# A two-layer recurrence: two of four k tiles of the recurrent product in bf16 parts, x Wx + b added behind the transpose

## The chip, the core and the metric

The kernel runs on one core of a Trainium2 chip. The metric is the device time of one execution in microseconds (us).

## The reference

Input x is (8, 1024, 512) in f32: 8 sequences (B) of 1,024 steps (T) and width 512 (D). Two layers, each with its own Wx and Wh (512 x 512) and b, start from the same state cond (8 x 512):

```
def step(h_prev, xw_t):
    h_next = jnp.tanh(h_prev @ Wh + xw_t)      # xw_t = x_t @ Wx + b
    return (h_next, h_next)
x = x + layer0(x, cond, Wx0, Wh0, b0)
x = x + layer1(x, cond, Wx1, Wh1, b1)
return x
```

So 2 x 1,024 steps depend on one another within each layer; layer 1's input at step n needs layer 0's output at step n.

## The kernel before

Everything is f32 but the bias. The width of 512 is held as 128 partitions times 4 k tiles (KC = 4). Layer 1 runs 8 steps (LAG) behind layer 0, so in a "slot" s the kernel does step s of layer 0 and step s - 8 of layer 1; 1,016 of the 1,032 slots hold both layers, 8 at each end hold one.

**TensorE.** The small operand, h or x of four steps (32 columns: 4 steps x 8 sequences), is loaded into a 32-column group of the array; the 128 columns of a piece of W stream past it. The four column groups g take the four quarters of the output width and write PSUM partitions 32g to 32g + 31, so four matmuls, one for each g, run side by side. `project` (L184) computes x Wx of four steps at once, one k tile in each call (L192), and for k = 0 first adds the bias with one bf16 matmul for each g (L188); it starts the accumulation in a PSUM bank `ps`, of which each layer has two. `recur` (L199) waits for the last h (L203) and adds h Wh into the same bank, with 16 matmuls (4 k tiles x 4 groups, L206); h of step n - 1 stands in a window of 32 columns of which 24 are zeros, placed so that it lands in the rows of step n. `slot` (L211) writes the order out: recur of layer 0, a projection step, one or more projection steps of layer 1 by a table (L30), recur of layer 1.

**VectorE** waits for the recurrence (`turn`, L275) and transposes the whole bank in 32 x 32 blocks into `zt` (L277). Every four slots it also does two sums of four steps each: `sum_mid`, x + h of layer 0, which is layer 1's input (L282), and `sum_out`, x_mid + h of layer 1, the output (L287). **ScalarE** waits for the transpose and applies tanh to the 32 columns of its step, which gives h (`tanh`, L244, L257). **GpSimd** only clears h at the start (L271). **SP** (SyncE) moves 64 KB pieces of four steps: x for TensorE, x for VectorE, and the output (L165 to L175). The programs of TensorE, ScalarE and VectorE are loops over eight slots (`stretches`, L54) with the first and last slots written out; the class `Edge` keeps their semaphore counts. At the start VectorE splits the bias in three bf16 parts (L305 to L315).

## Time and profile before

| | |
|---|---|
| median of 3 runs | 2303.1 us (2302.53 to 2303.13) |
| profiled execution, its own time | 2300.86 us |
| its span in the trace | 2299.1 us |
| TensorE busy / its weight loads | 99% / 99% |
| VectorE / ScalarE / GpSimd busy | 33% / 21% / 0% |
| granted TensorE clock | 1.0 of full speed |
| HBM traffic | 24 GB/s over the span |

PE is TensorE's matmul, PEld its weight load, DVE is VectorE, ACT ScalarE, POOL GpSimd, SP SyncE. Matmuls are pipelined and their ends are modelled, so that TensorE is "busy" does not say that it works at its peak. A line of a kernel is written L206.

### The profile page before, as it was taken

The numbers are of one execution on the slowest core, as the hardware profiler recorded it, in microseconds if no ns is written. First come the engines' busy times: TensorE is split into PE (matmuls) and PEld (weight loads), VectorE is DVE, ScalarE is ACT, GpSimd is POOL, SyncE is SP. The second block draws the span as 40 slices with busy tenths as digits, with TensorE's granted clock in tenths as the row PEclk, the third lists the DMA queues.
The fourth block names the chain that finished last, engine by engine and source line by source line (L and its number), as shares of the span: only waits on it lengthen the run. The fifth ranks groups of instructions, "written<-read, shape, count | busy, mean of one in ns | idle before, by whom it ended". The sixth has DMA issues, their size and how long they took to land.

```text
span 2299.1 us, 176381 instructions
## 1 busy us (share of the span) xinstructions
PE 2272.2 (99%) x83968; PEld 2264.9 (99%) x83968; DVE 759.5 (33%) x2573; ACT 471.4 (21%) x2049; POOL 2.2 (0%) x6
## 2 busy tenths in 40 slices
PE   6999999999999999999999999999999999999998
PEld 6999999999999999999999999999999999999998
DVE  2333333333333333333333333333333333333332
ACT  1222222222222222222222222222222222222221
POOL 0000000000000000000000000000000000000000
PEclk9999999999999999999999999999999999999999
DMA  2000000000000000000000000000000000000000
GB/s 100 26 22 23 22 23 22 23 22 23 22 23 22 23 22 23 22 23 22 23 22 23 22 23 22 23 22 23 22 23 22 23 22 23 22 23 22 23 22 18
DMA packets 112545, 55.61 MB, mean 24 GB/s; under 512 B 13440, under 2 KB 111744, under 8 KB 112000
## 3 DMA queue, kind: packets, MB, share of 16 engines
q1 hardware_dynamic: 112368, 54.08, 7.9%
q10 hardware_dynamic: 144, 1.05, 0.1%
q8 instruction: 25, 0.41, 0.1%
q14 instruction: 8, 0.07, 0.0%
HBM read 38.31 MB, written 16.78 MB: 24 GB/s over the span
## 4 chain that ended last, share of the span: by engine, by line
PE 99%; DVE 0%; DMA 0%; ACT 0%; issue 0%; SPq 0%; ACTq 0%; DVEq 0%
PE ps L206 78%; PE ps L192 20%; PE ps L188 1%; DMA bias<-b_in 0%; DVE zt L277 0%; ACT h L257 0%; DVE bias_rest L307 0%; DVE bias_last L311 0%; DVE bias_part L315 0%; DVE bias_part L313 0%; DVE bias_part L309 0%; SPq L156 0%; SPq L155 0%; SPq L154 0%; DVE x_out L287 0%
## 5 line engine op out<-in xcount | busy, mean ns | idle before, releaser
L206 PE MATMUL ps<-wh,h 128*32 128x128 f32 x65536 | 2103.9, 273 | 7.8 <-ACT h L257 7.4
L206 PEld LDWEIGHTS ps<-wh,h 128*32 128x32 f32 x65536 | 1956.7, 110 | 14.5 <-ACT h L257 11.9
L277 DVE STREAM_TRANSPOSE zt<-ps 128x128 f32<-128x128 f32 x2048 | 649.0, 317 | 1489.3 <-PE ps L206 1489.3
L257 ACT ACTIVATE h<-zt 128x32 f32<-128x32 f32 x2048 | 470.1, 230 | 1824.1 <-DVE zt L277 1824.1
L192 PE MATMUL ps<-wx,x_pe 128*32 128x128 f32 x8192 | 563.2, 273 | 0.0
L192 PE MATMUL ps<-wx,x_mid 128*32 128x128 f32 x8192 | 478.1, 273 | 0.0
L192 PEld LDWEIGHTS ps<-wx,x_pe 128*32 128x32 f32 x8192 | 383.0, 110 | 0.2
L192 PEld LDWEIGHTS ps<-wx,x_mid 128*32 128x32 f32 x8192 | 339.5, 110 | 0.0
L188 PE MATMUL ps<-bias_part,ones 128*32 128x128 bf16 x2048 | 198.2, 219 | 16.1 <-DVE bias_part L315 16.1
L188 PEld LDWEIGHTS ps<-bias_part,ones 128*32 128x32 bf16 x2048 | 114.0, 97 | 16.1 <-DVE bias_part L315 16.1
L282 DVE TENSOR_TENSOR x_mid<-x_dve,h 128x128 f32<-128x128 f32 x256 | 74.8, 292 | 37.4 <-DVE x_out L287 0.2
L287 DVE TENSOR_TENSOR x_out<-x_mid,h 128x128 f32<-128x128 f32 x256 | 63.9, 250 | 0.3 <-ACT h L257 0.3
L307 DVE TENSOR_TENSOR bias_rest<-bias 128x512 f32<-128x512 f32 x2 | 1.4, 694 | 9.6 <-DMA bias<-b_in 9.5
L271 POOL MEMSET h<- 128x1096 f32 x2 | 2.0, 1011 | 0.3 <-POOLq L344 0.3
L257 ACT ACT_TABLE_LOAD x1 | 1.3, 1283 | 1.2 <-PEq L344 1.2
L311 DVE TENSOR_TENSOR bias_last<-bias_rest 128x512 f32<-128x512 f32 x2 | 1.3, 673 | 0.0
L313 DVE COPY bias_part<-bias_rest 1x512 bf16<-1x512 bf16 x2 | 0.8, 418 | 0.1
L315 DVE CAST bias_part<-bias_last 1x512 bf16<-1x512 f32 x2 | 0.8, 418 | 0.0
L309 DVE COPY bias_part<-bias 1x512 bf16<-1x512 bf16 x2 | 0.8, 407 | 0.0
L317 DVE MEMSET ones<- 128x32 bf16 x1 | 0.1, 85 | 0.8 <-PEq L344 0.8
L318 DVE MEMSET bias_part<- 128x256 uint32 x1 | 0.3, 272 | 0.0
L319 DVE MEMSET bias_part<- 128x256 uint32 x1 | 0.3, 272 | 0.0
(4 smaller groups left out, 0.4 us busy)
## 6 DMA issues: line engine op xcount, KB each, us to landing
x_pe<-x_t SPq DMA_DIRECT2D x256, 64.0 KB, 1.8
x_dve<-x_t SPq DMA_DIRECT2D x256, 64.0 KB, 1.9
out_t<-x_out SPq DMA_DIRECT2D x256, 64.0 KB, 1.7
wx<-wx_in SPq DMA_DIRECT2D x2, 1024.0 KB, 7.6
wh<-wh_in ACTq DMA_DIRECT2D x1, 1024.0 KB, 5.7
wh<-wh_in SPq DMA_DIRECT2D x1, 1024.0 KB, 9.3
bias<-b_in SPq DMA_DIRECT2D x2, 256.0 KB, 8.2
h<-cond_t SPq DMA_DIRECT2D x2, 16.0 KB, 8.1
```

The lines of the kernel that those rows point to most:

```text
L188: pe.matmul(bank(l, c, g), ones[:, :], bias_part[l][:, g * P:(g + 1) * P], start=True, stop=False, skip_group_check=True, tile_position=(0 ...
L192: mm = pe.matmul(bank(l, c, g), src, wx[l][:, k, g * P:(g + 1) * P], start=False, stop=False, skip_group_check=True, tile_position=(0, 32 ...
L206: mm = pe.matmul(bank(l, n // S4, g), h[l][:, at + k * ROWS:at + (k + 1) * ROWS], wh[l][:, k, g * P:(g + 1) * P], start=False, stop=k == K ...
L257: act.activation(h_of(l, n), src[:, :, off:off + B], ACT.Tanh).then_inc(done, 1)
L271: pool.memset(h[l][:, :], 0.0).then_inc(s_clear, 1)
L277: dve.transpose(zt[l][n % 2][:, :], ps[l][n // S4 % 2][:, 0:P]).then_inc(zt_done[l].sem, 1)
L282: dve.tensor_tensor(x_group(x_mid, c), x_group(x_dve, c), h_group(0, c), ALU.add).then_inc(mid_last if c == NG - 1 else mid_done.sem, 1)
L287: dve.tensor_tensor(x_group(x_out, c), x_group(x_mid, c), h_group(1, c), ALU.add).then_inc(out_own.sem, 1)
L307: dve.tensor_tensor(bias_rest[l][:, :], bias[l][:, :], upper(bias[l][:, :]), ALU.subtract).then_inc(s_bown, 1)
L309: dve.tensor_copy(bias_part[l][0:1, :], upper(bias[l][0:1, :]))
L311: dve.tensor_tensor(bias_last[l][:, :], bias_rest[l][:, :], upper(bias_rest[l][:, :]), ALU.subtract).then_inc(s_bown, 1)
L313: dve.tensor_copy(bias_part[l][32:33, :], upper(bias_rest[l][32:33, :]))
```

## The change

- **Two k tiles in bf16 parts.** For k = 0 and 1, Wh is split before the loop into three bf16 parts (`wh_part`: upper half of the number, upper half of the rest, last rest), and h of each step into three parts too. The parts of h stand beside each other in 24 columns (3 parts x 8 sequences) and are loaded together, as the upper halves of f32 words; the three parts of Wh stream past them in turn, which gives all nine products, in 24 rows of each group. k = 2 and 3 stay in f32 and run first, as soon as h is there; k = 2 with 32 columns (the columns behind the first 8 hold zeros there), which also starts all 32 rows, k = 3 with 8. TensorE waits a second time, for the parts (`split_done`), before the bf16 matmuls: 6 for each column group, 24 in a step, in the place of 8 f32 ones.
- **Own banks.** The recurrence accumulates in `ps_rec`, one bank for each layer, the projections in `ps_xw`, two for each layer.
- **Behind the transpose.** VectorE transposes the recurrence's bank into columns 8 to 39 of a slot of `zt`, and once per layer and four steps the projections' bank into columns 0 to 7 of four slots (`place`). A `tensor_reduce` (`total`) adds up four pieces of 8 columns: x Wx + b and the three rows of parts. ScalarE's tanh reads the sum `z`.
- **Splitting h** on VectorE: `rest` (h less its upper half) after tanh, `last` (rest less its upper half), for two k tiles of 8 columns: 16 elements each. VectorE's order of these operations is written out in `slot`.
- **The two sums** go from VectorE to GpSimd. GpSimd also makes the parts of layer 1's Wh at the start; VectorE and ScalarE make those of layer 0.
- **Projections** are spread two k tiles a slot, one behind each layer's recurrence. **SP** has the store ahead of the x_dve load, and loads layer 1's Wh earlier. VectorE's and ScalarE's loops are written out; only TensorE keeps one.

The core of the diff:

```diff
+KB = 2
+PARTS = 3
...
+LAYERS = (0, 1)
...
-        wh = [sb(f"wh{l}", [P, KC, D]) for l in LAYERS]
+        wh = [sb(f"wh{l}", [P, KC * D]) for l in LAYERS]
+        wh_rest = [sb(f"wh_rest{l}", [P, KB * D]) for l in LAYERS]
+        wh_part = [sb(f"wh_part{l}", [P, PARTS, KB * D], BF16) for l in LAYERS]
...
-        h = [sb(f"h{l}", [P, 2 * HALF + B]) for l in LAYERS]
-        zt = [[sb(f"zt{l}_{i}", [P, P]) for i in range(2)] for l in LAYERS]
...
+        h = [sb(f"h{l}", [P, RING * P]) for l in LAYERS]
+        zt = [sb(f"zt{l}", [P, RING * KC * SLOT]) for l in LAYERS]
+        z = [[sb(f"z{l}_{i}", [P, COLS]) for i in range(2)] for l in LAYERS]
...
-        ps = [[ctx.enter_context(nc.psum_tensor(f"ps{l}_{i}", [P, 512], F32)) for i in range(2)] for l in LAYERS]
+        ps_rec = [psum(f"ps_rec{l}") for l in LAYERS]
+        ps_xw = [[psum(f"ps_xw{l}_{i}") for i in range(2)] for l in LAYERS]
...
+        h_done = [sem(f"h_done{j}") for j in range(2)]
+
+        def h_count(l, n):
+
+            s = n + LAG * l
+            steps = [(m, t) for t in range(s - s % S4, s + 1) for m in LAYERS if number(m, t) is not None]
+            return h_done[s // S4 % 2], steps.index((l, s)) + 1
...
-        def window(n):
-
-            w = n % RING
-            return w // 4 * HALF + w % 4 * P + (32 if w % 4 == 3 else 0), B * ((n + 1) % 4)
+        def h_step(l, n):
+            return h[l][:, n % RING * P:(n % RING + 1) * P].rearrange("p (k c) -> p k c", k=KC)
 
         def h_of(l, n):
-            at, off = window(n)
-            return h[l][:, at:at + P].rearrange("p (k r) -> p k r", r=ROWS)[:, :, off:off + B]
+            return h_step(l, n)[:, :, 0:B]
+
+        def h_bits(l, n):
+
+            return h[l][:, n % RING * P:(n % RING + 1) * P].bitcast(BF16).rearrange(
+                "p (k c two) -> p k c two", k=KC, two=2)[:, :, :, 1]
 
...
+            sp.dma_start(wh[1][:, :], weights[1][1].rearrange("p k d -> p (k d)")).then_inc(s_wh[1], DMA)
...
-            sp.dma_start(wh[1][:, :, :], weights[1][1]).then_inc(s_wh[1], DMA)
             for c in range(1, NG + 4):
-                if c + 1 in range(2, NG):
-                    sp.wait_ge(s_x_pe_used, c)
+                if 2 <= c + 1 < NG:
+                    sp.wait_ge(proj_done[0], c)
                     load(x_pe, x_pe_loaded, c + 1)
-                if c in range(2, NG):
-                    sp.wait_ge(s_x_mid_seen, c - 1)
+                if c >= 4:
+                    sp.wait_ge(out_done, c - 3)
+                    sp.dma_start(out[:, c - 4, :], x_out[c % 2][:, :]).then_inc(out_free[c % 2], DMA)
+                if 2 <= c < NG:
+                    sp.wait_ge(mid_done, c - 1)
                     load(x_dve, x_dve_loaded, c)
-                if c >= 4:
-                    sp.wait_ge(s_out_done, c - 3)
-                    sp.dma_start(out[:, c - 4, :], x_out[c % 2][:, :]).then_inc(out_free[c % 2].sem, DMA)
...
+                bank = ps_xw[l][c % 2]
                 if k == 0:
...
                 for g in range(QG):
-                    mm = pe.matmul(bank(l, c, g), src, wx[l][:, k, g * P:(g + 1) * P], start=False, stop=False,
-                                   skip_group_check=True, tile_position=(0, 32 * g))
...
+                    mm = pe.matmul(rows(bank, g, ROWS), src, wx[l][:, k, g * P:(g + 1) * P], start=False,
+                                   stop=k == KC - 1, skip_group_check=True, tile_position=(0, 32 * g))
+                if k == KC - 1:
+                    mm.then_inc(proj_done[l], 1)
 
             def recur(l, n):
 
-                at, _ = window(n - 1)
-                if n:
-                    h_done.wait(pe, h_at[l, n - 1])
-                for k in range(KC):
+
+                if n == 0:
+                    pe.wait_ge(s_hinit, 2 * DMA)
+                else:
+                    pe.wait_ge(*h_count(l, n - 1))
+                for k in range(KB, KC):
+                    m = ROWS if k == KB else B
                     for g in range(QG):
-                        mm = pe.matmul(bank(l, n // S4, g), h[l][:, at + k * ROWS:at + (k + 1) * ROWS],
-                                       wh[l][:, k, g * P:(g + 1) * P], start=False, stop=k == KC - 1,
-                                       skip_group_check=True, tile_position=(0, 32 * g))
-                mm.then_inc(rec_done.sem, 1)
-
-            def slot(r):
-
+                        at = k * D + g * P
+                        pe.matmul(rows(ps_rec[l], g, m), h_step(l, n - 1)[:, k, 0:m], wh[l][:, at:at + P],
+                                  start=k == KB, stop=False, skip_group_check=True, tile_position=(0, 32 * g))
+                if n == 0:
+                    pe.wait_ge(s_hsplit, 2)
+                    pe.wait_ge(s_wpart[l], PARTS)
+                else:
+                    pe.wait_ge(split_done, SPLIT_AT[l, n - 1] - base)
+                for k in range(KB):
+                    for i in range(PARTS):
+                        for g in range(QG):
+                            at = k * D + g * P
+                            mm = pe.matmul(rows(ps_rec[l], g, PARTS * B), h_bits(l, n - 1)[:, k, 0:PARTS * B],
+                                           wh_part[l][:, i, at:at + P], start=False,
+                                           stop=k == KB - 1 and i == PARTS - 1, skip_group_check=True,
+                                           tile_position=(0, 32 * g))
+                mm.then_inc(rec_done, 1)
...
+            def projections(s, half):
+
+                l, k = s % S4 // 2, s % 2 * 2 + half
+                c = (s - 6) // S4 if l else s // S4 + 1
+                if 0 <= c < NG:
...
+                    project(l, c, k)
+
+            def slot(s):
+
+                if (n := number(0, s)) is not None:
+                    recur(0, n)
+                projections(s, 0)
+                if (n := number(1, s)) is not None:
+                    recur(1, n)
+                projections(s, 1)
...
-                        mid_done.wait(act, c + 1)
-                zt_done[l].wait(act, n + 1)
-                src = zt[l][n % 2][:, :].rearrange("p (k r) -> p k r", r=ROWS)
-                off = B * (n % S4)
-                done = h_last[l] if n == T - 1 else h_done.sem
-                act.activation(h_of(l, n), src[:, :, off:off + B], ACT.Tanh).then_inc(done, 1)
...
+                        act.wait_ge(mid_done, c + 1)
+                elif n % S4 == 0 and n >= RING:
+                    act.wait_ge(out_done, n // S4 - 1)
+                act.wait_ge(z_done, STEP_AT[l, n])
+                act.activation(h_of(l, n), z[l][n % 2][:, :].rearrange("p (k b) -> p k b", k=KC), ACT.Tanh).then_inc(
+                    h_count(l, n)[0], 1)
...
+                if s % S4 == 0 and s:
+                    done, count = h_count(*last)
+                    act.sem_inc(done, -count)
...
+            act.activation(wh_part[0][:, 0, :], upper(wh[0][:, 0:KB * D]), ACT.Copy).then_inc(s_wpart[0], 1)
+            act.wait_ge(s_wrest[0], 1)
+            act.activation(wh_part[0][:, 1, :], upper(wh_rest[0][:, :]), ACT.Copy).then_inc(s_wpart[0], 1)
...
+            def sum_mid(c):
+
+                pool.wait_ge(x_dve_loaded[c % 2], DMA * (c // 2 + 1))
+                if c >= 2:
+                    pool.wait_ge(out_done, c - 1)
+                pool.wait_ge(rest_done, STEP_AT[0, S4 * c + 3])
+                pool.tensor_tensor(x_group(x_mid, c), x_group(x_dve, c), h_group(0, c), ALU.add).then_inc(mid_done, 1)
...
+            def sum_out(c):
...
+                pool.wait_ge(mid_done, c + 1)
+                pool.wait_ge(rest_done, STEP_AT[1, S4 * c + 3])
+                pool.tensor_tensor(x_group(x_out, c), x_group(x_mid, c), h_group(1, c), ALU.add).then_inc(out_done, 1)
...
+            pool.wait_ge(s_wh[1], DMA)
+            full, rest = wh[1][:, 0:KB * D], wh_rest[1][:, :]
+            pool.tensor_tensor(rest, full, upper(full), ALU.subtract).then_inc(s_wrest[1], 1)
+            pool.tensor_copy(wh_part[1][:, 0, :], upper(full)).then_inc(s_wpart[1], 1)
+            pool.wait_ge(s_wrest[1], 1)
+            pool.tensor_copy(wh_part[1][:, 1, :], upper(rest)).then_inc(s_wpart[1], 1)
+            pool.tensor_tensor(wh_part[1][:, 2, :], rest, upper(rest), ALU.subtract).then_inc(s_wpart[1], 1)
...
+            def place(l, c):
...
+                dve.wait_ge(proj_done[l], c + 1)
+                dve.transpose(zt_group(l, c), ps_xw[l][c % 2][:, 0:P]).then_inc(xw_done[l], 1)
...
             def turn(l, n):
-                rec_done.wait(dve, rec_at[l, n])
-                dve.transpose(zt[l][n % 2][:, :], ps[l][n // S4 % 2][:, 0:P]).then_inc(zt_done[l].sem, 1)
-
...
+                dve.wait_ge(rec_done, STEP_AT[l, n])
+                dve.transpose(zt_of(l, n)[:, :, B:SLOT], ps_rec[l][:, 0:P]).then_inc(zt_done, 1)
+
+            def total(l, n):
+                if n % S4 == 0:
+                    dve.wait_ge(xw_done[l], n // S4 + 1)
+                dve.wait_ge(zt_done, STEP_AT[l, n])
+                dve.tensor_reduce(z[l][n % 2][:, :].rearrange("p (k b) -> p k b", k=KC),
+                                  zt_of(l, n)[:, :, 0:4 * B].rearrange("p k (i b) -> p k b i", b=B),
+                                  AX.X, ALU.add).then_inc(z_done, 1)
...
+            def rest(l, n):
+                step = h_step(l, n)
+                return dve.tensor_tensor(step[:, 0:KB, B:2 * B], step[:, 0:KB, 0:B], h_bits(l, n)[:, 0:KB, 0:B],
+                                         ALU.subtract)
...
+            def last(l, n):
+                step = h_step(l, n)
+                return dve.tensor_tensor(step[:, 0:KB, 2 * B:3 * B], step[:, 0:KB, B:2 * B],
+                                         h_bits(l, n)[:, 0:KB, B:2 * B], ALU.subtract)
+
+            def split_rest(l, n):
+                dve.wait_ge(*h_count(l, n))
+                rest(l, n).then_inc(rest_done, 1)
...
+            def split_last(l, n):
+                if n < T - 1:
+                    dve.wait_ge(rest_done, STEP_AT[l, n])
+                    last(l, n).then_inc(split_done, 1)
+
+            def slot(s):
+                a, b, b_before = number(0, s), number(1, s), number(1, s - 1)
+                if a is not None:
+                    turn(0, a)
+                if b_before is not None:
+                    split_last(1, b_before)
+                if a is not None:
+                    total(0, a)
+                    if s % S4 == 2 and s // S4 + 1 < NG:
+                        place(0, s // S4 + 1)
+                if s % S4 == 0 and s >= LAG and b is not None:
+                    place(1, b // S4)
+                if a is not None:
+                    split_rest(0, a)
+                if b is not None:
+                    turn(1, b)
+                if a is not None:
+                    split_last(0, a)
+                if b is not None:
+                    total(1, b)
+                    split_rest(1, b)
...
+            dve.wait_ge(s_wh[0], DMA)
+            w_full, w_rest = wh[0][:, 0:KB * D], wh_rest[0][:, :]
+            dve.tensor_tensor(w_rest, w_full, upper(w_full), ALU.subtract).then_inc(s_wrest[0], 1)
+            dve.wait_ge(s_hinit, 2 * DMA)
+            rest(0, -1)
+            rest(1, -1).then_inc(s_hsplit, 1)
+            dve.wait_ge(s_wrest[0], 1)
+            dve.tensor_tensor(wh_part[0][:, 2, :], w_rest, upper(w_rest), ALU.subtract).then_inc(s_wpart[0], 1)
+            dve.wait_ge(s_hsplit, 1)
```

## Rows read from the trace of the kernel before

**Rows 1.** The page, busy time of each engine: us, share of the span, instructions.

```profile
PE 2272.2 (99%) x83968; PEld 2264.9 (99%) x83968; DVE 759.5 (33%) x2573; ACT 471.4 (21%) x2049; POOL 2.2 (0%) x6
```

**Rows 2.** The page, chain that ended last: by engine, then by line.

```profile
PE 99%; DVE 0%; DMA 0%; ACT 0%; issue 0%; SPq 0%; ACTq 0%; DVEq 0%
PE ps L206 78%; PE ps L192 20%; PE ps L188 1%; DMA bias<-b_in 0%; DVE zt L277 0%; ACT h L257 0%; DVE bias_rest L307 0%; DVE bias_last L311 0%; DVE bias_part L315 0%; DVE bias_part L313 0%; DVE bias_part L309 0%; SPq L156 0%; SPq L155 0%; SPq L154 0%; DVE x_out L287 0%
```

**Rows 3.** Busy time of each engine in a stretch of two-layer slots (x: instructions).

```profile
core 0: us, PE busy (x) PEld busy (x) DVE busy (x) ACT busy (x) POOL busy (x), PEclk, DMA share, GB/s
1000.00:1100.00 100.00, 100.00 (x3719) 100.00 (x3714) 33.33 (x114) 20.66 (x90) 0.00 (x0) 1.00 0.08 22
```

**Rows 4.** The page, groups: xcount | busy, mean ns | idle before, releaser.

```profile
L206 PE MATMUL ps<-wh,h 128*32 128x128 f32 x65536 | 2103.9, 273 | 7.8 <-ACT h L257 7.4
...
L277 DVE STREAM_TRANSPOSE zt<-ps 128x128 f32<-128x128 f32 x2048 | 649.0, 317 | 1489.3 <-PE ps L206 1489.3
L257 ACT ACTIVATE h<-zt 128x32 f32<-128x32 f32 x2048 | 470.1, 230 | 1824.1 <-DVE zt L277 1824.1
L192 PE MATMUL ps<-wx,x_pe 128*32 128x128 f32 x8192 | 563.2, 273 | 0.0
...
L188 PE MATMUL ps<-bias_part,ones 128*32 128x128 bf16 x2048 | 198.2, 219 | 16.1 <-DVE bias_part L315 16.1
...
L282 DVE TENSOR_TENSOR x_mid<-x_dve,h 128x128 f32<-128x128 f32 x256 | 74.8, 292 | 37.4 <-DVE x_out L287 0.2
...
L307 DVE TENSOR_TENSOR bias_rest<-bias 128x512 f32<-128x512 f32 x2 | 1.4, 694 | 9.6 <-DMA bias<-b_in 9.5
L271 POOL MEMSET h<- 128x1096 f32 x2 | 2.0, 1011 | 0.3 <-POOLq L344 0.3
```

**Rows 5.** Timeline of TensorE, matmuls begun by 26.79, 26.81 and 26.87: start, us.

```profile
26.79 0.22 PE L188 MATMUL ps<-bias_part,ones 128*32 128x128 bf16 x1
...
26.79 0.24 PE L188 MATMUL ps<-bias_part,ones 128*32 128x128 bf16 x4
...
26.84 0.29 PE L192 MATMUL ps<-wx,x_pe 128*32 128x128 f32 x4
```

**Rows 6.** Timeline of VectorE in a slot with both sums: start us, us, engine.

```profile
1002.40 0.32 DVE L277 STREAM_TRANSPOSE zt<-ps 128x128 f32<-128x128 f32 x1 [1.05 <-PE ps L206]
1002.64 0.25 DVE L287 TENSOR_TENSOR x_out<-x_mid,h 128x128 f32<-128x128 f32 x1
1003.04 0.29 DVE L282 TENSOR_TENSOR x_mid<-x_dve,h 128x128 f32<-128x128 f32 x1
1003.28 0.32 DVE L277 STREAM_TRANSPOSE zt<-ps 128x128 f32<-128x128 f32 x1
```

**Rows 7.** Timeline of VectorE at the start, splitting the bias.

```profile
10.98 0.69 DVE L307 TENSOR_TENSOR bias_rest<-bias 128x512 f32<-128x512 f32 x1 [9.54 <-DMA bias<-b_in]
11.59 0.41 DVE L309 COPY bias_part<-bias 1x512 bf16<-1x512 bf16 x1
11.93 0.67 DVE L311 TENSOR_TENSOR bias_last<-bias_rest 128x512 f32<-128x512 f32 x1
12.63 0.42 DVE L313 COPY bias_part<-bias_rest 1x512 bf16<-1x512 bf16 x1
```

**Rows 8.** Timeline of the last slots, layer 1 alone.

```profile
2291.38 1.08 PE L206 MATMUL ps<-wh,h 128*32 128x128 f32 x32 [0.70 <-ACT h L257]
2292.53 0.32 DVE L277 STREAM_TRANSPOSE zt<-ps 128x128 f32<-128x128 f32 x1 [1.29 <-PE ps L206]
...
2294.31 0.32 DVE L277 STREAM_TRANSPOSE zt<-ps 128x128 f32<-128x128 f32 x1 [1.46 <-PE ps L206]
...
2296.09 0.32 DVE L277 STREAM_TRANSPOSE zt<-ps 128x128 f32<-128x128 f32 x1 [1.46 <-PE ps L206]
2296.44 0.23 ACT L257 ACTIVATE h<-zt 128x32 f32<-128x32 f32 x1 [1.55 <-DVE zt L277]
2296.70 0.29 DVE L287 TENSOR_TENSOR x_out<-x_mid,h 128x128 f32<-128x128 f32 x1 [0.29 <-ACT h L257]
```

**Rows 9.** The page, DMA issues: xcount, KB each, median us to landing.

```profile
x_dve<-x_t SPq DMA_DIRECT2D x256, 64.0 KB, 1.9
```

More of the change, by code:

```diff
@@ L233, in _, with turn, taken @@
+            def slot(s):
[5 more added lines that the diff above has]
+                projections(s, 1)
+            def turn(r):
+                for s in range(RING * r, RING * (r + 1)):
+                    slot(s)
+            def taken(r):
+                return SPLIT_AT[1, RING * r - 2 - LAG]
             pe.wait_ge(s_bsplit, 2)
@@ L238, in _ @@
             pe.wait_ge(s_wh[0], DMA)
-            pe.wait_ge(s_hinit, 2 * DMA)
-            stretches(pe, slot, [h_done])
+            for r in range(FIRST):
+                turn(r)
+            base = taken(FIRST)
+            pe.sem_inc(split_done, -base)
+            with pe.Fori(0, AFTER - FIRST, 1):
+                turn(FIRST)
+                pe.sem_inc(split_done, base - taken(FIRST + 1))
+            base = taken(AFTER)
+            for r in range(AFTER, END):
+                turn(r)
         @block.scalar
```

181 lines of the change are left out of this document (71 added, 110 removed).

## The prediction

> **What bounds the kernel now.** I read the page's busy times first: TensorE is busy for 99% of the span, VectorE 33%, ScalarE 21% [rows 1]. The chain that ended last agrees: 99% TensorE, nearly all of it the recurrence's own matmuls [rows 2]. Busy time of a pipelined engine proves little, so the third reading is a rate. In a middle stretch TensorE issues 3,719 matmul records in 100 us [rows 3], one per 26.89 ns. A program matmul in f32 shows as two records (65,536 of them for 1,024 steps x 2 layers x 16 [rows 4]), so a slot (a step of each layer) has 64 of the recurrence, 16 of the projections and 2 of the bias: 82 records, 82 x 26.89 = **2.205 us**. Four column groups of the array work side by side; I count in "quads" (the four matmuls of one k tile, one for each group). A bf16 quad is followed by the next f32 one after 0.05 us (26.79 to 26.84) [rows 5]; I take 0.056. An f32 quad is then (2.205 - 0.5 x 0.056)/10 = **0.218 us**. The other engines wait: VectorE sat 1,489 us for the recurrence and ScalarE 1,824 us for the transpose [rows 4]. So TensorE's work is the bound, and what the change takes from it counts until the chain of the other engines is longer.
>
> **What TensorE does after.** Of four f32 quads a step, two go (k = 0, 1) and 2 x 3 bf16 quads come. Per slot: 4 x 0.218 leaves, 12 x 0.056 comes, a saving of 0.872 - 0.672 = 0.20. TensorE's own slot is 6 x 0.218 + 12.5 x 0.056 = **2.01 us**, against 2.205. Bounds for the bf16 quad: 0.053 from below and, from above, 4 x 0.0269 = 0.108, if a bf16 matmul took as long to issue as an f32 record [rows 3]. I take 0.056 because it is the same instruction. The row against an issue limit is that all four bf16 matmuls have started within 0.02 us, and four f32 ones have within 0.07 us of the first [rows 5]. But this is a burst of four, out of a queue that had time to fill; twenty-four in a row are not in this trace.
>
> By a rule of the Trainium skill ("TensorE: Matmul & The Clock Gate", Wait — 56ns, not 53.3ns?) matmul starts never come closer than about 25 ns however short they are. Applied to every matmul, a bf16 quad would take 0.100 us and TensorE's slot 6 x 0.218 + 12.5 x 0.1 = 2.56 us. The trace does not bear it out across column groups, by the row just named; within one group it may hold and costs nothing.
>
> **What comes onto the chain behind TensorE.** Before, a step ends with transpose (0.317) and tanh (0.229); now VectorE has four operations a step: transpose, a reduce over four 8-wide pieces, and two subtractions for the parts. It runs them in a fixed order: transpose 0, last part 1, reduce 0, first rest 0 (which waits for tanh 0), transpose 1, last part 0, reduce 1, first rest 1 (which waits for tanh 1). Everything behind a waiting rest stands still, so **two tanh round trips lie in series on VectorE** in each slot. That is the new rival of TensorE, and I sum half of it:
> - Transpose 0.317 [rows 6]. The last part of the other layer issues 0.24 behind its start (x_out starts 0.24 behind the transpose) [rows 6] and the reduce must wait for the transpose anyway: hidden.
> - The reduce's own-engine wait: 0.03 (a subtraction of 0.67 started at 11.93, its reader at 12.63) [rows 7].
> - Reduce, 128 elements in: no row. The nearest is an add of 128 elements, 0.25 when queued behind another and 0.29 when started out of a wait [rows 6]. I take 0.29. Upper bound 0.42, if its 32-byte steps cost a second pass (0.133, the 128 elements at VectorE's pace: 384 more elements cost 694 - 292 ns, 1.05 each [rows 4]).
> - VectorE to ScalarE 0.033, tanh 0.229, ScalarE to VectorE 0.03 (transpose 2296.09, tanh 2296.44, x_out 2296.70) [rows 8].
> - First rest, 16 elements, until the transpose behind it may issue: 0.24 for 128 elements less 112 x 1.05 ns = 0.12. Between 0.09 (the fixed share of the long subtractions: 0.61 between two starts less 512 x 1.05 ns, plus 16 elements) [rows 7] and 0.17 (no overlap: 0.29 - 0.12).
> Sum: 0.317 + 0.03 + 0.29 + 0.033 + 0.229 + 0.03 + 0.12 = 1.05; twice gives **2.10 us a slot**. With the low values (reduce 0.25, rest 0.09) it is 1.96, with 0.17 it is 2.20.
>
> The placing of x Wx + b (one more transpose per layer and four slots) issues between reduce and rest, into the 0.29 us in which VectorE waits for tanh; it holds VectorE for 0.24: nothing. Without that cover it would cost 0.5 x 0.24 = 0.12 us a slot. The two sums leave VectorE's order and go to GpSimd: on VectorE they had no price while TensorE was the bound, so nothing is gained.
>
> **The loop through TensorE** also has to fit. From a transpose 0 to the next: half a round (1.05), transpose 1 holds VectorE 0.24, last part 0.13, to TensorE 0.04, six quads 0.34, then the tail of the last matmul 0.166 + 0.02 (219 ns recorded, 53 of it streaming) [rows 4] and 0.07 to VectorE (32 records end at 2292.46, transpose 2292.53) [rows 8]. 2.06 us, 0.04 below the round. TensorE meanwhile does its 2.01 us of work in the order f32 part, wait, bf16 part, projection; the f32 part and the projection of the other layer stand behind the wait for the parts, and are just enough to fill it. Three loops of 2.01, 2.06 and 2.10 interlock, so any mis-sized term moves the slot.
>
> **Queues and other waits.** SP issues the same three transfers per four slots, with the store now ahead of the x_dve load; a landing takes 1.9 us [rows 9] and the load is needed some two slots (4 us) later: nothing, and a slot more if both were doubled. ScalarE gets a reset of a counter every four slots and a wait for the output sum four slots old: it is idle 79% [rows 1], nothing. GpSimd's sums are due a slot later (projection of layer 1, and a wait of tanh 0): nothing below 1 us each. Loops of VectorE and ScalarE are written out; I price this at nothing: the instructions are of the same kinds, and both engines are mostly idle.
>
> **Ends.** In 16 slots only one layer runs, and there the whole chain shows: 1.78 us now (transposes at 2292.53 and 2294.31) [rows 8]. After: 0.317 + 0.03 + 0.29 + 0.033 + 0.229 + 0.03, rest 0.17, wait 0.03, last 0.17, 0.04, six quads 0.34, 0.186, 0.07 = 1.94. 16 x 0.16 = 3 us. Start: VectorE makes rests of wh0 before its first transpose (two subtractions over 1,024 elements, about 1.2 us each by [rows 7]) while TensorE does its first projections (2 us): 1 us more. GpSimd has some 15 us for wh1.
>
> **Sum**, against the profiled execution's 2300.9 us (the median of the runs is 0.1% above it): 1,016 two-layer slots x (2.10 - 2.205) = -107, +3, +1: **2198 us**.
>
> **Rivals.**
> - **B, GpSimd in VectorE's way.** GpSimd's two adds are released by the rest of the fourth step, exactly when VectorE comes to its subtractions. The trace has no GpSimd add; its price lies between VectorE's 0.25 [rows 6] and the 1.01 us of a GpSimd memset of 1,096 elements [rows 4]; I take 0.4, nearer the small size. If an add holds up the next subtraction until it ends, the first costs about 0.3 us and the second 0 to 0.4, per four slots: 0.07 to 0.17 a slot, 2.17 to 2.27 us, **2265 to 2370 us**. It decides from a sum of 4 x 0.105 = 0.42 us per four slots on: above it the kernel is slower than before. For it: the order of the releases. Against: no row shows the two engines at once.
> - **A, issue.** bf16 matmuls issue no faster than f32 records: 98 x 0.0269 = 2.64 us a slot, 2301 + 1016 x 0.43 + 4 = **2740 us**. Against it, the burst of rows 5.
> - **C, the reduce's stride** costs the second pass, 0.133 twice a slot on VectorE: 2.37, **2470 us**.
> - **D, VectorE's small operations are cheaper** (1.96): then TensorE's 2.01 decides, 2301 - 1016 x 0.19 + 4 = **2110 us**.
> - **E**: the waits inside a step eat the saving and no more, **2301**.
>
> The Trainium skill ("SBUF — State Buffer", Who interferes with whom) says that a VectorE instruction with two SBUF inputs and a GpSimd one that reads SBUF exclude each other for the whole instruction. That is rival B's mechanism; no row here shows it.
>
> **Chances.** Forecast 0.44, D 0.12, B 0.24 (its half below 2296 counts as faster, a tenth of it as the same, the rest slower), C 0.08, A 0.09, E 0.03. About 0.2% (4.6 us) is what a measurement can tell from no change. Faster: 0.44 + 0.12 + 0.11 = 0.67; same 0.02 + 0.03 = 0.05; slower 0.11 + 0.08 + 0.09 = 0.28. The range takes forecast, D and B: **2090 to 2370**. The forecast's own is 2130 to 2265.
>
> **What would show it.** Right: slots of 2.10 us, VectorE at 75 to 85% busy, its idle time ending on tanh, TensorE with short gaps at the wait for the parts; bf16 records of 13 to 14 ns spacing. B: subtractions of much more than 0.18 us, or late starts, every fourth slot beside a GpSimd add. A: TensorE without gaps and slots of 2.6 us. C: a reduce near 0.42 us. D: no gaps on TensorE and slots of 2.01. I am wrong outright if the granted clock, 1.0 now [rows 3], falls to the lower level in the gaps.

## The result, and the profile after

The changed kernel takes **2440.5 us** (median of 4 runs, 2440.0 to 2444.6) against 2302.8 us for the kernel before on the same chip (4 runs): a ratio of **1.060** [1.0585, 1.0621]. It is 6% slower, where the forecast was 2198 us, within 2090 to 2370.

The page of the changed kernel, from its parts on busy time and the chain, and the groups that the prediction priced (L207 and L218 are the f32 and bf16 matmuls of the recurrence, L349 the transpose, L355 the reduce, L361 the rest, L366 the last part, L345 the placing of x Wx + b, L323 and L316 the sums on GpSimd):

```profile
PE 2388.5 (98%) x100352; PEld 1722.8 (71%) x100352; DVE 1837.7 (75%) x8721; ACT 474.5 (19%) x2051; POOL 244.8 (10%) x522
...
DVE 64%; ACT 18%; PE 11%; issue 6%; ACTq 0%; DMA 0%; DVEq 0%; SPq 0%; POOLq 0%
...
L207 PE MATMUL ps_rec<-wh,h 128*32 128x128 f32 (+1 forms) x32768 | 1325.7, 279 | 22.0 <-ACT h L286 15.4
L218 PE MATMUL ps_rec<-wh_part,h 128*24 128x128 bf16 x49152 | 1061.9, 221 | 6.8 <-issue 4.6
...
L286 ACT ACTIVATE h<-z 128x32 f32<-128x32 f32 x2048 | 471.1, 230 | 1946.9 <-DVE z L355 1946.9
L355 DVE TENSOR_REDUCE z<-zt 128x32 f32<-128x128 f32 x2048 | 786.2, 384 | 27.3 <-DVE zt L349 3.2
L361 DVE TENSOR_TENSOR h<-h 128x16 f32<-128x16 f32 x2050 | 375.4, 183 | 538.7 <-ACT h L286 501.7
L349 DVE STREAM_TRANSPOSE zt<-ps_rec 128x128 f32<-128x128 f32 x2048 | 631.3, 308 | 24.7 <-PE ps_rec L218 24.6
...
L323 POOL TENSOR_TENSOR x_out<-x_mid,h 128x128 f32<-128x128 f32 x256 | 117.9, 460 | 2127.9 <-DVE h L361 2127.9
L366 DVE TENSOR_TENSOR h<-h 128x16 f32<-128x16 f32 x2048 | 270.8, 132 | 0.5
```

TensorE still shows 98% busy, about as in [rows 1], but in the two-layer slots it is no longer the bound: the chain has gone from 99% TensorE [rows 2] to 64% VectorE and 18% ScalarE. That is how little "busy" says of a pipelined engine. The reduce takes 384 ns, and VectorE's longest waits are for tanh (501.7 us in front of the rest). The same view as [rows 3], busy time by stretch, with the ends of the span in it:

```profile
1000.00:1100.00 100.00, 99.47 (x4204) 71.51 (x4193) 76.15 (x366) 19.79 (x86) 10.11 (x22) 1.00 0.08 21
...
25.00:30.00 5.00, 4.10 (x100) 3.18 (x96) 1.76 (x7) 0.46 (x2) 0.00 (x0) 0.51 0.06 16
...
2430.00:2442.00 12.00, 5.55 (x148) 4.02 (x136) 3.97 (x15) 0.92 (x4) 0.64 (x2) 0.56 0.05 12
```

A slot now has 98 records, so it takes 98 x 100/4204 = **2.331 us**, against 2.205 before. 1,016 slots x 0.126 = 128 us of the 144 us by which the span grew (2442.8 less 2299.1). The other 16 us lie at the start and in the one-layer slots at both ends, where the granted clock is in part about half of full speed.

VectorE's timeline of three half rounds (a half round is one layer's share of a slot, from one transpose L349 to the next), and below it ScalarE's tanh in the same place:

```profile
1002.70 0.31 DVE L349 STREAM_TRANSPOSE zt<-ps_rec 128x128 f32<-128x128 f32 x1
1002.93 0.13 DVE L366 TENSOR_TENSOR h<-h 128x16 f32<-128x16 f32 x1
1003.04 0.38 DVE L355 TENSOR_REDUCE z<-zt 128x32 f32<-128x128 f32 x1
1003.72 0.17 DVE L361 TENSOR_TENSOR h<-h 128x16 f32<-128x16 f32 x1 [0.30 <-ACT h L286]
1003.82 0.31 DVE L349 STREAM_TRANSPOSE zt<-ps_rec 128x128 f32<-128x128 f32 x1
1004.05 0.13 DVE L366 TENSOR_TENSOR h<-h 128x16 f32<-128x16 f32 x1
1004.23 0.39 DVE L355 TENSOR_REDUCE z<-zt 128x32 f32<-128x128 f32 x1
1004.54 0.31 DVE L345 STREAM_TRANSPOSE zt<-ps_xw 128x128 f32<-128x128 f32 x1
1004.91 0.24 DVE L361 TENSOR_TENSOR h<-h 128x16 f32<-128x16 f32 x1
1005.08 0.30 DVE L349 STREAM_TRANSPOSE zt<-ps_rec 128x128 f32<-128x128 f32 x1
1005.31 0.13 DVE L366 TENSOR_TENSOR h<-h 128x16 f32<-128x16 f32 x1
1005.48 0.38 DVE L355 TENSOR_REDUCE z<-zt 128x32 f32<-128x128 f32 x1
```
```profile
1003.46 0.23 ACT L286 ACTIVATE h<-z 128x32 f32<-128x32 f32 x1 [0.89 <-DVE z L355]
1004.65 0.23 ACT L286 ACTIVATE h<-z 128x32 f32<-128x32 f32 x1 [0.96 <-DVE z L355]
1005.96 0.23 ACT L286 ACTIVATE h<-z 128x32 f32<-128x32 f32 x1 [1.08 <-DVE z L355]
```

The first half round is a plain one and takes 1.12 us: reduce 0.34 behind the transpose, tanh 0.42 behind the reduce, rest 0.26 behind tanh, next transpose 0.10 behind the rest. The second takes 1.26: the reduce starts 0.18 behind the last part instead of 0.11, and the rest takes 0.24 instead of 0.17, with a GpSimd add beside it. In the third, tanh starts 0.10 us behind the end of the reduce, not 0.04. Four slots have the half rounds 1.12, 1.26, 1.24, 1.16, 1.12, 1.12, 1.11 and 1.17: 9.30 us, of which 0.42 is above eight plain ones.

### The profile page after: what moved, and what is told of

Same layout as the page of the kernel before. It is cut to its first block, busy times and chain, and to the rows that moved or that the text cites. A ratio compares the mean times of both kernels' runs of the same rounds, so it can differ in the third digit from the quotient of the medians.

```text
span 2442.8 us, 215227 instructions
## 1 busy us (share of the span) xinstructions
PE 2388.5 (98%) x100352; PEld 1722.8 (71%) x100352; DVE 1837.7 (75%) x8721; ACT 474.5 (19%) x2051; POOL 244.8 (10%) x522
## 3 DMA queue, kind: packets, MB, share of 16 engines
q10 hardware_dynamic: 144, 1.05, 0.1%
## 4 chain that ended last, share of the span: by engine, by line
DVE 64%; ACT 18%; PE 11%; issue 6%; ACTq 0%; DMA 0%; DVEq 0%; SPq 0%; POOLq 0%
DVE z L355 29%; ACT h L286 18%; DVE zt L349 17%; DVE h L361 14%; PE ps_rec L207 5%; DVE h L366 4%; PE ps_rec L218 4%; PE ps_xw L191 2%; ACTq L285 0%; DMA bias<-b_in 0%; PE ps_xw L187 0%; DVE bias_part L408 0%; DVE wh_rest L421 0%; DVE bias_part L410 0%; DVEq L354 0%
## 5 line engine op out<-in xcount | busy, mean ns | idle before, releaser
L207 PE MATMUL ps_rec<-wh,h 128*32 128x128 f32 (+1 forms) x32768 | 1325.7, 279 | 22.0 <-ACT h L286 15.4
L218 PE MATMUL ps_rec<-wh_part,h 128*24 128x128 bf16 x49152 | 1061.9, 221 | 6.8 <-issue 4.6
L207 PEld LDWEIGHTS ps_rec<-wh,h 128*32 128x32 f32 (+1 forms) x32768 | 733.6, 99 | 395.2 <-ACT h L286 337.5
L218 PEld LDWEIGHTS ps_rec<-wh_part,h 128*24 128x24 bf16 x49152 | 697.2, 92 | 297.9 <-DVE h L366 51.8
L286 ACT ACTIVATE h<-z 128x32 f32<-128x32 f32 x2048 | 471.1, 230 | 1946.9 <-DVE z L355 1946.9
L355 DVE TENSOR_REDUCE z<-zt 128x32 f32<-128x128 f32 x2048 | 786.2, 384 | 27.3 <-DVE zt L349 3.2
L361 DVE TENSOR_TENSOR h<-h 128x16 f32<-128x16 f32 x2050 | 375.4, 183 | 538.7 <-ACT h L286 501.7
L349 DVE STREAM_TRANSPOSE zt<-ps_rec 128x128 f32<-128x128 f32 x2048 | 631.3, 308 | 24.7 <-PE ps_rec L218 24.6
L191 PE MATMUL ps_xw<-wx,x_mid 128*32 128x128 f32 x8192 | 402.9, 273 | 2.0 <-issue 2.0
L191 PE MATMUL ps_xw<-wx,x_pe 128*32 128x128 f32 x8192 | 402.9, 274 | 0.7 <-issue 0.7
L323 POOL TENSOR_TENSOR x_out<-x_mid,h 128x128 f32<-128x128 f32 x256 | 117.9, 460 | 2127.9 <-DVE h L361 2127.9
L366 DVE TENSOR_TENSOR h<-h 128x16 f32<-128x16 f32 x2048 | 270.8, 132 | 0.5
L345 DVE STREAM_TRANSPOSE zt<-ps_xw 128x128 f32<-128x128 f32 x512 | 156.7, 306 | 0.1
L316 POOL TENSOR_TENSOR x_mid<-x_dve,h 128x128 f32<-128x128 f32 x256 | 117.4, 458 | 55.0 <-DVE h L361 21.4
```

Of the source, the lines that this page charges most:

```text
L191: mm = pe.matmul(rows(bank, g, ROWS), src, wx[l][:, k, g * P:(g + 1) * P], start=False, stop=k == KC - 1, skip_group_check=True, tile_posi ...
L207: pe.matmul(rows(ps_rec[l], g, m), h_step(l, n - 1)[:, k, 0:m], wh[l][:, at:at + P], start=k == KB, stop=False, skip_group_check=True, til ...
L218: mm = pe.matmul(rows(ps_rec[l], g, PARTS * B), h_bits(l, n - 1)[:, k, 0:PARTS * B], wh_part[l][:, i, at:at + P], start=False, stop=k == K ...
L286: act.activation(h_of(l, n), z[l][n % 2][:, :].rearrange("p (k b) -> p k b", k=KC), ACT.Tanh).then_inc(h_count(l, n)[0], 1)
L316: pool.tensor_tensor(x_group(x_mid, c), x_group(x_dve, c), h_group(0, c), ALU.add).then_inc(mid_done, 1)
L323: pool.tensor_tensor(x_group(x_out, c), x_group(x_mid, c), h_group(1, c), ALU.add).then_inc(out_done, 1)
```

## The experiments

Three things had to be told apart: what the reduce costs and why, what the longer half rounds are, and whether TensorE would have kept its part of the forecast.

**1. Four pieces side by side (contig).** The layout of `zt` is turned so that the reduce reads adjacent words:

```diff
-  dve.transpose(zt_of(l, n)[:, :, B:SLOT], ...)
+  dve.transpose(zt_pieces(l, n).rearrange("p k b i -> p k i b")[:, :, 1:5, :], ...)
-  ... zt_of(l, n)[:, :, 0:4 * B].rearrange("p k (i b) -> p k b i", b=B)
+  ... zt_pieces(l, n)[:, :, :, 0:4]          # [p, k, b, i], i innermost in memory
```

> The changed kernel with another layout of zt: the transposes write each column's five pieces beside each other (steps of 20 bytes on the write), so that the reduce reads its four pieces from adjacent words instead of in steps of 32 bytes. Theory S (the reduce takes 384 ns because of its stride): the reduce falls to about 290 ns, the half round from 1.11 to 1.02 us, the slot from 2.33 to about 2.14 to 2.16, the time to about 2260 us, below the kernel before. Theory F (384 ns is what a reduce of 128 elements to 32 costs, however it reads): the reduce stays at 370 to 400 ns and the time at 2440 us. A third way: the strided write makes the transpose longer (above 317 ns) and takes back what the reduce gives.

2455.9 us, ratio 1.066 [1.0647, 1.0682]. The two groups on its page:

```profile
L354 DVE STREAM_TRANSPOSE zt<-ps_rec 128x128 f32<-128x128 f32 x2048 | 847.9, 414 | 22.4 <-PE ps_rec L223 22.3
...
L360 DVE TENSOR_REDUCE z<-zt 128x32 f32<-128x128 f32 x2048 | 586.3, 286 | 82.7 <-DVE zt L354 3.6
```

Theory S is right about the reduce (286 ns, close to the 290 priced in the forecast), and the third way takes it back: the transpose, writing single words in steps of 20 bytes, goes from 308 to 414.

**2. Two pieces of four (half).** The sum leaves out two of the three part rows: the rests of h times Wh.

```diff
-  ... zt_of(l, n)[:, :, 0:4 * B] ...
+  ... zt_of(l, n)[:, :, 0:2 * B] ...
```

> The reduce adds two of the four pieces (x Wx + b and the first part row); the other two part rows are left out of the sum. 64 elements in. Theory S (stride, a cost per element of up to 2 ns): 384 - 64 x 2 = about 260 ns. Theory F1 (1.05 ns per element and a larger fixed cost): 384 - 67 = 317 ns. Theory F2 (the cost goes with the 32 outputs): 384 ns. The slot falls by twice what the reduce falls: to 2.08, 2.20 or 2.33 us, the time to 2190, 2305 or 2440 us.

2223.0 us, ratio 0.966 [0.9636, 0.9675]; the reduce:

```profile
L355 DVE TENSOR_REDUCE z<-zt 128x32 f32<-128x64 f32 x2048 | 454.7, 222 | 22.1 <-DVE zt L349 3.2
```

222 ns, less than any theory gave. 286 and 222 lie 64 elements at 1.0 ns apart: with two pieces in steps of 32 bytes the reduce costs no more per element than with adjacent words, with four in the same steps (384 - 286)/128 = 0.8 ns more. This sets the two pieces beside a value worked out from 1.0 ns an element, near the 1.05 of [rows 4]; no run has a reduce over two adjacent words. The stride alone is not it. And with a reduce of 222 the kernel is faster than before: the sign of the whole change can hang on this one instruction.

**3. No reduce (noreduce).** tanh reads the first part row from `zt`; x Wx + b and the other two part rows are left out.

```diff
-  act.wait_ge(z_done, ...);  act.activation(h_of(l, n), z[l][n % 2]..., ACT.Tanh)
+  act.wait_ge(zt_done, ...); act.activation(h_of(l, n), zt_of(l, n)[:, :, B:2 * B], ACT.Tanh)
```

> No reduce: tanh reads the first part row straight from the transposed bank; the x Wx + b and two part rows are left out of the sum. It takes 0.38 + 0.03 us from each half round. My account: VectorE's round is then 2 x 0.7, the loop through TensorE 1.8, and TensorE's own work decides, 2.01 us a slot: about 2110 to 2130 us, TensorE without gaps, bf16 matmuls 13 to 14 ns apart. Rival A (sustained bf16 matmuls issue more slowly than one every 14 ns): the slot stays above 2.1 us with TensorE never waiting.

2153.5 us. Busy time of a stretch, and the matmuls of one bf16 part with the f32 ones around them:

```profile
1000.00:1100.00 100.00, 99.97 (x4800) 88.11 (x4792) 60.74 (x317) 22.49 (x98) 11.12 (x25) 1.00 0.09 24
```
```profile
1001.88 0.62 PE L207 MATMUL ps_rec<-wh,h 128*32 128x128 f32 x16
1002.32 0.52 PE L218 MATMUL ps_rec<-wh_part,h 128*24 128x128 bf16 x24
1002.65 0.40 PE L191 MATMUL ps_xw<-wx,x_pe 128*32 128x128 f32 x8
```

98 x 100/4800 = 2.04 us a slot, against the 2.01 forecast for TensorE alone. 24 bf16 matmuls run from 1002.32 to 1002.65: about 14 ns each, 0.055 a quad. Rival A is out in the steady part. The time is some 30 us above my account, and 1,016 slots x 0.03 us are 30 us: the excess lies in the steady slots in the main, and not at the start. More than half of it is one pause: once in eight slots, which is the length of TensorE's loop, two neighbouring matmuls start 0.28 us apart instead of 0.10. That is 0.18/8 = 0.02 us a slot. The kernel before has no such pause.

**4. GpSimd without reads (nosum).** Both sums x + h are left out; memsets with the same waits stand in their place.

```diff
-  pool.tensor_tensor(x_group(x_mid, c), x_group(x_dve, c), h_group(0, c), ALU.add)
+  pool.memset(x_group(x_mid, c), 0.0)        # x_out in the same way
```

> GpSimd's two adds of four steps become memsets of the same tiles, with the same waits: the sums x + h are left out, GpSimd reads no SBUF. Theory B (GpSimd's reads exclude VectorE's subtractions): the two half rounds of 1.26 and 1.24 us per four slots fall to 1.11, the slot from 2.33 to 2.26, the time by 1016 x 0.07 = 71 us and by some 3 us at the start less nothing, to about 2370 us. If the long half rounds come from something else in those slots (semaphore work, the store's DMA): 2440 us.

2423.8 us, ratio 1.053 [1.0512, 1.0547]: 17 us, not 71. The long half rounds are mostly not GpSimd's; without its reads they still take 1.17 to 1.26 us on average.

**5. Other spacings (pitch9, pitch12, block4).** Three layouts, to see what the four pieces' distance does.

```diff
-SLOT = 5 * B
+SLOT = 5 * PITCH        # PITCH = 9 or 12: pieces 36 or 48 bytes apart
```

> The changed kernel with zt's five pieces 9 words (36 bytes) apart instead of 8; everything else as it is, the transposes still write runs of 8 words. The reduce took 384 ns with four pieces in steps of 32 bytes, 222 ns with two of them, 286 ns with four adjacent words. Theory K (steps of exactly 32 bytes over four pieces collide): at 36 bytes the reduce takes about 290 ns, the half round 1.02 us, the time about 2250 us. Theory L (four pieces in four different 16-byte stretches cost it, whatever the step): 384 ns and 2440 us again.

> As pitch9, with the pieces 12 words (48 bytes) apart. Theory K: about 290 ns and 2250 us, unless the collision is one of 16-byte multiples, when it stays; theory L: 384 ns and 2440 us.

> Another layout of zt: runs of 4 words (16 bytes), the five pieces' runs beside each other, so that the four pieces the reduce reads are 16 bytes apart, in 64 adjacent bytes. Theory L: the reduce stays near 384 ns. Theory K: near 290 ns. The transposes write runs of 4 words instead of 8: between 309 ns (no price) and the 414 ns of runs of one word. With 290 and 309 the time is about 2250 us, with 384 and 360 it is 2500 us.

2436.3, 2426.3 and 2434.3 us. The reduce of pitch12 and of block4, and block4's transpose:

```profile
L356 DVE TENSOR_REDUCE z<-zt 128x32 f32<-128x128 f32 x2048 | 770.2, 376 | 27.4 <-DVE zt L350 3.2
```
```profile
L360 DVE TENSOR_REDUCE z<-zt 128x32 f32<-128x128 f32 x2048 | 780.3, 381 | 27.5 <-DVE zt L354 3.2
...
L354 DVE STREAM_TRANSPOSE zt<-ps_rec 128x128 f32<-128x128 f32 x2048 | 629.2, 307 | 21.1 <-PE ps_rec L223 20.9
```

Theory K falls: 16, 32, 36 or 48 bytes, the reduce takes 376 to 384 ns. Theory L stands, four pieces in four places (16-byte stretches) cost it, and the write of runs of 4 words is free. That left the runs of 2 words, where the four elements of one sum are 8 bytes apart and lie in two such places.

**6. The order of two waits (swap).** Where tanh or the reduce waits for two things, the late one is now waited for first.

```diff
+  act.wait_ge(z_done, STEP_AT[l, n])
   ...  act.wait_ge(mid_done, c + 1)         # or x_pe_loaded, out_done
-  act.wait_ge(z_done, STEP_AT[l, n])
   act.activation(...)
+  dve.wait_ge(zt_done, STEP_AT[l, n])
   if n % S4 == 0: dve.wait_ge(xw_done[l], n // S4 + 1)
-  dve.wait_ge(zt_done, STEP_AT[l, n])
   dve.tensor_reduce(...)
```

> Only the order of two waits is changed, where an instruction has two: ScalarE waits for the reduced sum first and for the long-finished x load, x_mid or x_out second (three of eight tanh in four slots); VectorE's reduce waits for its transpose first and for the long-placed x Wx + b second (two of eight). In the trace of the changed kernel tanh starts 0.09 us behind the reduce in these cases and 0.03 us in the others. Theory W (the wait written last is executed by the sequencer in its own time, after the long one has passed): with the late one first, the 0.06 us goes: 5 x 0.06 = 0.3 us per four slots, 76 us in all, about 2365 us. Theory V (a second wait costs 0.06 us in either order): 2440 us.

2373.5 us, ratio 1.031 [1.0292, 1.0327]: **67 us** for a change of order. Theory W stands. The chain of waits of the changed kernel names the price, pieces in order of time (start, us, what), around the tanh at 1005.96 shown above:

```profile
1005.88 0.02 issue
1005.90 0.02 ACTq L285
1005.91 0.04 issue
1005.96 0.24 ACT h L286
```

With the waits swapped, the instruction of its own is the other wait (for x_out at 1002.95, right behind the tanh before), and it is over long before the sum is there. In this run GpSimd's adds stand out instead (VectorE, then GpSimd):

```profile
1002.41 0.13 DVE L366 TENSOR_TENSOR h<-h 128x16 f32<-128x16 f32 x1
1002.53 0.38 DVE L355 TENSOR_REDUCE z<-zt 128x32 f32<-128x128 f32 x1
1002.83 0.30 DVE L345 STREAM_TRANSPOSE zt<-ps_xw 128x128 f32<-128x128 f32 x1
...
1003.20 0.32 DVE L361 TENSOR_TENSOR h<-h 128x16 f32<-128x16 f32 x1
```
```profile
1002.43 0.46 POOL L323 TENSOR_TENSOR x_out<-x_mid,h 128x128 f32<-128x128 f32 x1 [8.00 <-DVE h L361]
...
1003.03 0.46 POOL L316 TENSOR_TENSOR x_mid<-x_dve,h 128x128 f32<-128x128 f32 x1
```

The first add starts 0.02 us behind the last part and meets only a reduce and transposes, which do not mind. The second covers the rest, which takes 0.32 us instead of 0.17 and ends at 1003.52, 0.03 behind the end of the add (1003.49). That is the rule and not this one case: between 100 and 2000 us, every subtraction of over 0.2 us ends 0.027 to 0.035 us behind the end of a GpSimd add, 204 of them in the changed kernel and 210 here. VectorE's subtraction is held until the add is done.

**7. GpSimd's second sum one step later (swaplate).** On top of the swapped waits.

```diff
-  pool.wait_ge(rest_done, STEP_AT[0, S4 * c + 3])
+  pool.wait_ge(rest_done, STEP_AT[0, min(S4 * c + 4, T - 1)])
```

> The two waits swapped as in the run before (2373.5 us), and GpSimd's sum for layer 1 released by layer 0's rest of the next step, so that its add starts when VectorE's last subtraction has begun and ends before the next one. In the run with the waits swapped one rest in eight took 0.32 instead of 0.17 us, beside a GpSimd add. Theory B (GpSimd's reading add and VectorE's two-input subtraction exclude each other): that 0.14 us per four slots goes, 256 x 0.14 = 36 us, about 2338 us, and all rests take 0.17 to 0.18. Otherwise 2373 us.

2345.7 us, ratio 1.019 [1.0172, 1.0203]: 28 us less than swap, of the 36 expected; the rest's mean falls from 193 ns (swap) to 176.

**8. Runs of two words (pair2), and all three together (best).** `SLOT = 6 * B`, and `zt` as [k, b/2, piece, 2]:

```diff
-  dve.transpose(zt_of(l, n)[:, :, B:SLOT], ...)
+  dve.transpose(zt_pieces(l, n).rearrange("p k t i b -> p k i t b")[:, :, 1:5, :, :], ...)
-  ... zt_of(l, n)[:, :, 0:4 * B].rearrange("p k (i b) -> p k b i", b=B)
+  ... zt[l][:, at:at + KC * SLOT].rearrange("p (t i b) -> p t b i", i=6, b=2)[:, :, :, 0:4]
```

> zt in runs of 2 words, the pieces' runs beside each other: the four pieces that a sum reads lie in 8 adjacent words. Between the layouts measured so far: runs of 8 or 4 words (reduce 381 to 384 ns, transpose 308) and single words (reduce 286, transpose 414). If the price of each goes with the number of 16-byte stretches in use, the reduce reads two, as in the run with two pieces of four, and falls to 290 ns; the transposes write 8 bytes in each, so 309 (no price) to 360 ns. The time is 2250 us with 290 and 309, 2350 us with 290 and 360, 2440 us if the two only trade places again.

2280.8 us, ratio 0.991 [0.9891, 0.9928]: the layout alone turns the result round, though only to 0.9% below the kernel before.

```profile
L354 DVE STREAM_TRANSPOSE zt<-ps_rec 128x128 f32<-128x128 f32 x2048 | 636.0, 311 | 24.5 <-PE ps_rec L223 24.4
L360 DVE TENSOR_REDUCE z<-zt 128x32 f32<-128x128 f32 x2048 | 587.0, 287 | 27.6 <-DVE zt L354 3.2
```

The reduce reads at full pace and the transpose pays nothing.

> All three: runs of 2 words, waits swapped, GpSimd's sum released later. If the terms add up: 2338 us less what the pair layout saves alone. With a reduce of 290 and a transpose of 309 the half round is 1.02 and the slot 2.04, where TensorE's own work (2.04 in the run without the reduce) is the bound as well: about 2160 us, below the kernel before by 6%. With a transpose of 360 about 2240 us. If the layout gives nothing: 2338 us.

**2199.6 us**, ratio **0.955** [0.954, 0.9566]: below both kernels, with nothing left out. It is TensorE's again, by the chain, and runs near the floor of experiment 3 (98 x 100/4708 = 2.08 us a slot):

```profile
PE 97%; DVE 1%; issue 1%; DMA 0%; ACT 0%; SPq 0%; POOLq 0%; DVEq 0%
```

That it lands on the 2198 us of the forecast is chance: the forecast had VectorE as the bound and none of these three edits. It stays 40 us above the 2160 that I expected. Its timeline shows a last part on VectorE beside GpSimd's first add:

```profile
1007.42 0.38 DVE L371 TENSOR_TENSOR h<-h 128x16 f32<-128x16 f32 x1
```
```profile
1007.32 0.46 POOL L328 TENSOR_TENSOR x_out<-x_mid,h 128x128 f32<-128x128 f32 x1 [6.69 <-DVE h L366]
```

The add starts 0.10 before the last part, and no longer just behind it, and the last part takes 0.38 us instead of 0.13: it ends 0.03 behind the add. TensorE's bf16 matmuls wait for it:

```profile
1007.86 0.34 PEld L223 LDWEIGHTS ps_rec<-wh_part,h 128*24 128x24 bf16 x24 [0.30 <-DVE h L371]
```

The trace gives the price. This happens once in eight slots (123 times; four slots later, at 1015.82, the last part starts 0.02 before the add and takes 0.13), and each time the bf16 matmuls start 0.19 us late: 23 us in all. The whole distance to noreduce is 2.088 - 2.046 = 0.042 us a slot, by the transposes, or 43 us. The rest of it is spread: in seven of the sixteen half rounds of eight slots the bf16 matmuls start some 0.02 us late, by TensorE's start times. A version that releases the first add later too was not run.

**9. One more turn written out (first3)**, on top of best. Until about 90 us TensorE is slow in every version of the changed kernel: 35 records per us, with idle stretches that the trace puts down to its own issue.

```diff
-FIRST = 2
+FIRST = 3
```

> The kernel of the run before (2199.6 us) with three turns of eight slots of TensorE's program written out ahead of its loop instead of two. Up to about 88 us, the end of the loop's first pass, TensorE does 34 to 36 matmul records per us in every version, whatever bounds it afterwards, with idle stretches of 0.5 to 1 us that nothing else explains; afterwards 43 to 48. Theory F (code that runs for the first time is supplied no faster than that, code that the loop repeats is): the slow stretch grows by one turn, to about 110 us, and the time by 8 slots x 98 records x (1/35 - 1/47) us = 6 us, to about 2205 us. Theory G (the slow stretch is a matter of the start, such as the other engines' programs or the loads): it ends at 88 us as before and the time stays within 1 us.

2203.0 us (2201.9 to 2205.5), 3.4 us more. One stretch behind 90 us, first3 and then best:

```profile
90.00:105.00 15.00, 11.38 (x524) 9.75 (x516) 8.65 (x46) 2.41 (x11) 0.91 (x2) 1.00 0.08 22
```
```profile
90.00:105.00 15.00, 15.00 (x728) 12.49 (x724) 11.17 (x62) 3.46 (x15) 1.14 (x3) 1.00 0.08 23
```

35 records per us against 48.5: the slow stretch moves with the end of the first pass through the loop. That is theory F. The price is half of what I worked out, and by the times alone it would not be clear: the two ratios are 0.9553 [0.954, 0.9566] and 0.9575 [0.9559, 0.9591].

The DMA views of best name a queue of the kind "instruction", first from 42 to 100 us, then from 100 to 2100 us (packets, MB, share):

```profile
q8 instruction: 12, 0.20, 1.5%
```
```profile
q8 instruction: 1, 0.02, 0.0%
```

These are packets of 16 KB. They come every 3.3 to 4.0 us until 84 us, and in step with them TensorE pauses 0.7 to 1.4 us after every 128 matmul records (at 62.2, 66.1, 70.2 and 74.0 us for instance). Once the loop repeats, the packets stop, and so do these pauses; in first3 both go on until some 105 us. That TensorE waits for these packets is read from their timing; the trace does not say whose they are. The kernel before takes its first pass at the same pace of packets, but its pauses there are 0.4 us at most, because it needs only 37 records per us.

## Why the prediction was wrong

**What held.** TensorE's work fell about as costed: 2.04 us a slot where nothing else binds (noreduce), for 2.01. The rule of the Trainium skill ("TensorE: Matmul & The Clock Gate", Wait — 56ns, not 53.3ns?) with about 25 ns between matmul starts, which would have made it 2.56, does not hold across column groups: about 14 ns, twenty-four in a row. VectorE's fixed order with two tanh round trips in series did become the bound; 64% and 18% of the chain are its two engines, and its plain half round is the loop that I summed. Placing x Wx + b is hidden: with the waits swapped, the half round with a placement (from 1006.78 on) is as long as the others, 1.11 us.

**The step that failed: "Reduce, 128 elements in: no row ... I take 0.29".** It took 0.384. The upper bound of 0.42 was right, and its reason, a price on the 32-byte steps, was near; I gave it a chance of 0.08 because I took the add's row as the nearest, though that add reads runs of 8 words and the reduce jumps between four places. The plain half round came out at 1.11 instead of 1.05 (reduce +0.09, the rest's hold on VectorE 0.10 and not 0.12, and small change). Twice 0.06 x 1,016 = 122 us, which is more than the 107 that the forecast had as gain: this term alone cancels it. With the layout that brings the reduce to 287 ns, and nothing else changed, the kernel takes 2280.8 us (pair2), 160 us less.

**A term that was missing: the second wait.** I wrote of ScalarE's new wait "it is idle 79% [rows 1], nothing". An idle engine hides work that is done before the awaited thing comes, not work that is queued behind it: 0.06 us for each of five instructions in four slots, 67 us by experiment 6. It stood in the kernel before: there too some tanh wait for two things.

**Rival B.** The mechanism is as I wrote it: a subtraction that meets an add on GpSimd is held until the add ends, and ends 0.03 us behind it (experiment 6). The rule of the Trainium skill ("SBUF — State Buffer", Who interferes with whom) agrees. The price was too high: 17 us (nosum), or 0.017 us a slot, where the least I gave it was 0.07; with the waits swapped about 28 us (swaplate). I had let the first add block a subtraction; it starts as that subtraction starts, and only the second meets one, when the add is already partly done. At the start a copy stretches too, VectorE and GpSimd in the changed kernel (the same copy took 0.42 us at 13.14 and takes 2.00 here):

```profile
15.67 2.00 DVE L408 COPY bias_part<-bias_rest 1x512 bf16<-1x512 bf16 x1
```
```profile
15.10 2.29 POOL L329 TENSOR_TENSOR wh_rest<-wh 128x1024 f32<-128x1024 f32 x1 [12.53 <-DMA wh<-wh_in]
```

**The ends.** I priced them at 4 us; they cost 16. The first transpose of the recurrence starts at 24.6 us and not 19.9; copies and subtractions like this one, held up by GpSimd, are a part of that. The 8 one-layer slots at the start take 6 us more than before, what follows the last two-layer slot 5 us more. Such a slot takes 2.8 us where the clock is low (transposes at 27.49 and 30.30) and 2.06 where it is 1.0 (40.96 and 43.02), against the 1.94 that I summed, of which the reduce is 0.1. And TensorE's first pass through its code, in the first 16 two-layer slots, costs some 7 us, which no step of mine had.

**The account:** 2198 forecast, +122 (plain half rounds), +107 (long half rounds: 67 for the waits, 28 for the second add, 12 that no run tells apart), +7 (first pass) and +12 (ends) give 2446, against 2444.6 us of the profiled execution and a median of 2440.5. It is no closer than its rounding: 0.01 us in a half round is 20 us.

## What to carry to other kernels

- When work moves from the bound engine to one that is 33% busy, sum the new loop of that engine in its program order, waits included, and treat every instruction of a new kind in it as the largest risk: here one reduce, off by 0.09 us, decided the sign.
- The price of the small reduce here went with how many separate places it read for one sum. Before giving up on a layout, look for the one between: runs of 2 words were free to write and fast to read, where 1 and 8 each failed on one side.
- Of two waits before an instruction on the critical loop, write the one that comes last first.
